# Two selects over every other column in place of a select in runs of two, with a new order of the steps

## The chip, the cores and the metric

One core of one Trainium2 chip runs the whole program. The metric is the device time in microseconds. The engines named below are PE (TensorE), DVE (VectorE), ACT (ScalarE), POOL (GpSimd) and SP (the queue that issues the DMAs).

## The reference

A gated delta-rule attention layer, then a mixture-of-experts layer, each followed by a residual and a layer norm. The input is 4 sequences of 512 tokens with 256 features. There are 16 key heads and 32 value heads of width 128.

```python
mixed = silu(causal_conv(hidden @ w_qkv, conv_w))        # 4 taps
q, k, v = split(mixed);  q, k repeated for 2 value heads each
g = -exp(A_log) * softplus(a + dt_bias);  beta = sigmoid(b)
q, k = l2norm(q) * DK ** -0.5, l2norm(k)
for t in range(S):                                       # per value head
    state = state * exp(g[t])
    delta = (v[t] - k[t] @ state) * beta[t]
    state = state + outer(k[t], delta)
    o[t] = q[t] @ state
o = rmsnorm(o * silu(hidden @ w_z)) * norm_gamma
x = layernorm(x + o @ w_out)
x = layernorm(x + moe(rmsnorm(x)))                       # 8 experts, top 2, and a shared one
```

## The kernel before

The recurrence over time is done in chunks of 128 tokens. Within a chunk it becomes the inverse of a 128 x 128 triangular matrix, and between chunks a 128 x 128 state is carried. A *body* is one key head of one sequence: 4 chunks times 2 value heads, which are 8 *cells*. There are 16 x 4 = 64 bodies (`BODIES`). The mixture of experts comes after them.

A body goes through these steps. `proj` multiplies the input with the weights of q, k and v; `tap` (ACT) and `conv` (DVE, twelve per body) are the four taps of the convolution, `silu` its activation. `ktp` and `vtp` are transposes on PE, `squares` and `kn` give the norms, `gate` and `zs` the output gate. `products` forms k k^T and q k^T. `diag` (POOL) and `scan` (DVE) make the decay matrix, and `m` and `p` (DVE) multiply the products with it.

The matrix m32T is then inverted for all 8 cells together. `mhi` (POOL, two halves) writes its fp16 copy mhiT with ones on the diagonal. `pairs` (POOL) writes the inverse of the 2 x 2 blocks on the diagonal to XT, and `x0` (DVE) transposes XT to X. Six levels follow (block sizes 2 to 64, i = 0 to 5): `join i` on PE and on DVE gives N, `growx i` on PE and ACT gives the new X, and XT is made anew by a DVE transpose (`turned`, levels 0 and 1) or by `growt` on PE and ACT (levels 2 to 5). `newton`, `res`, `finish` and `tt` correct the result once and give TT; `mlo` (POOL) is the low half of the matrix for that.

With TT the four chunks are gone through in order: `read`, `rhs`, `solve`, `u`, `write`, `s`, and `out` for the output. Then `og`, `power`, `pow`, `ogs`, `turn`, `project` and `acc` gate, normalise and project the output and add it up.

Work of three bodies is interleaved. The order is written out by hand in `ORDER`, one list per engine; an entry is (step, i, ahead). `rounds` goes through a list once for every k, and the entry works on body k + ahead. Each engine executes its list strictly in order, and semaphores hold the engines together. So a step that waits holds up everything behind it in its engine's list. One pass of a list is called a round here.

The names and lines that matter below: `conv` L1125, `proj` L870, `gate` L894, `products` L904, `join` L914 on PE and L1161 on DVE, `growx` L924 and L1075, `growt` L930 and L1078, `m` L1137, `mhi` L796, `pairs` L810 and L815, `x0` L1152, `turned` L1155, `mlo` L802 and L804, `squares` L1052, `solve` L965, `write` L975, `rhs` L1179.

Of the kernel before, what the change touches and what calls it, by code (L numbers as in the profile page):

```python
# [17 lines left out]
CELLS = CH * VH  # L18
# [10 lines left out]

ORDER = {  # L30
    "tensor": [
        ("read", 2, 0), ("growx", 0, 1), ("gate", 1, 1), ("gate", 2, 1), ("join", 1, 1), ("gate", 3, 1),
        ("growx", 1, 1), ("proj", 0, 2), ("proj", 1, 2), ("join", 2, 1), ("solve", 2, 0), ("proj", 2, 2),
        ("growx", 2, 1), ("growt", 2, 1), ("proj", 3, 2), ("join", 3, 1), ("write", 2, 0), ("out", 0, 0),
        ("growx", 3, 1), ("ktp", 0, 2), ("read", 3, 0), ("growt", 3, 1), ("join", 4, 1), ("out", 1, 0),
        ("growx", 4, 1), ("solve", 3, 0), ("growt", 4, 1), ("out", 2, 0), ("join", 5, 1), ("out", 3, 0),
        ("growx", 5, 1), ("growt", 5, 1), ("proj", 4, 2), ("newton", 0, 1), ("ktp", 1, 2), ("proj", 5, 2),
        ("newton", 1, 1), ("finish", 0, 1), ("proj", 6, 2), ("finish", 1, 1), ("proj", 7, 2), ("solve", 0, 1),
        ("products", 0, 2), ("write", 0, 1), ("products", 1, 2), ("turn", 0, 0), ("read", 1, 1), ("turn", 1, 0),
        ("project", 0, 0), ("project", 1, 0), ("solve", 1, 1), ("project", 2, 0), ("project", 3, 0), ("vtp", 0, 2),  # L40
        ("write", 1, 1), ("vtp", 1, 2), ("join", 0, 2), ("gate", 0, 2),
    ],
    "scalar": [
        ("u", 1, 0), ("silu", 2, 1), ("silu", 3, 1), ("vals", 0, 1), ("vals", 1, 1), ("growx", 0, 1), ("zs", 0, 1),
        ("growx", 1, 1), ("zs", 1, 1), ("tap", 0, 2), ("u", 2, 0), ("growx", 2, 1), ("growt", 2, 1), ("silu", 0, 2),
        ("tap", 1, 2), ("growx", 3, 1), ("squares", 0, 2), ("growt", 3, 1), ("kraw", 0, 2), ("u", 3, 0),
        ("growx", 4, 1), ("growt", 4, 1), ("power", 0, 0), ("growx", 5, 1), ("silu", 1, 2), ("growt", 5, 1),
        ("squares", 1, 2), ("tap", 2, 2), ("power", 1, 0), ("u", 0, 1), ("tap", 3, 2), ("turn", 0, 0), ("turn", 1, 0),
    ],
    "vector": [  # L50
        ("join", 2, 1), ("conv", 0, 2), ("conv", 1, 2), ("conv", 2, 2), ("join", 3, 1), ("s", 2, 0), ("conv", 3, 2),
        ("join", 4, 1), ("rhs", 3, 0), ("og", 0, 0), ("conv", 4, 2), ("conv", 5, 2), ("join", 5, 1), ("scan", 0, 2),
        ("scan", 1, 2), ("res", 0, 1), ("og", 1, 0), ("res", 1, 1), ("tt", 0, 1), ("tt", 1, 1), ("conv", 6, 2),
        ("conv", 7, 2), ("conv", 8, 2), ("s", 0, 1), ("conv", 9, 2), ("m", 0, 2), ("m", 1, 2), ("rhs", 1, 1),
        ("conv", 10, 2), ("conv", 11, 2), ("p", 0, 2), ("p", 1, 2), ("x0", 0, 2), ("acc", 0, 0), ("s", 1, 1),
        ("join", 0, 2), ("rhs", 2, 1), ("turned", 0, 2), ("join", 1, 2), ("acc", 1, 0), ("turned", 1, 2),
    ],
    "pool": [
        ("eq", 0, 1), ("mlo", 0, 1), ("qe", 0, 1), ("keys", 0, 1), ("kn", 0, 2), ("diag", 0, 2), ("pow", 0, 0),
        ("ogs", 0, 0), ("ogs", 1, 0), ("mhi", 0, 2), ("mhi", 1, 2), ("pairs", 0, 2),  # L60
    ],
}

# [10 lines left out]
def build_kernel(nc, x_rows, x_cols, w_heads, w_ab, conv_w, dt_bias, a_log, gamma, w_out,  # L74
                 rms_w, router_w, gate_up, down, tri, levels16, neg_mask, ident16, iota8, exponents, out):
    ctx = ExitStack()
    with ctx:
# [3 lines left out]
        def sem(name):  # L81
            return ctx.enter_context(nc.semaphore(name))
# [18 lines left out]
        acc = sb("acc", [P, TILES, D])  # L101
# [7 lines left out]
        conv = sb("conv", [P, GROUPS, SEQ])  # L109
# [20 lines left out]
        mhiT = sb("mhiT", [P, CELLS, P], F16)  # L130
# [591 lines left out]
        def _(pool):  # L722
# [18 lines left out]
            def run(name, i, n):  # L741
# [42 lines left out]
                elif name == "qe":  # L784
                    pool.wait_ge(s_silu, 4 * n + 2)
                    pool.wait_ge(s_ec[p], 16 * (n // 2 + 1))
                    if n > 1:
                        pool.wait_ge(s_pup, 2 * (n - 1))
                    pool.tensor_tensor(qE[:, p, VH:].rearrange("p (c v) n -> p c v n", v=VH),
                                       qT[:, p, P:].rearrange("p (c n) -> p c n", n=P).unsqueeze(2).broadcast_to([P, CH - 1, VH, P]),  # L790
                                       ecb[:, p, VH * P:].rearrange("p (c v n) -> p c v n", v=VH, n=P), ALU.mult).then_inc(s_qe, 1)
                elif name == "mhi":
                    pool.wait_ge(s_m, 2 * n + i + 1)
                    if n > 0:
                        pool.wait_ge(s_resp, 2 * n)
                    pool.affine_select(out=half(mhiT, i), in_=half(m32T, i), compare_op=ALU.not_equal, fill=1.0,  # L796
                                       base=0, pattern=[[0, 4], [-1, P]], channel_multiplier=1).then_inc(s_mhi, 1)
                elif name == "mlo":
                    pool.wait_ge(s_mhi, 2 * n + 2)
                    if n > 0:  # L800
                        pool.wait_ge(s_newp, 2 * n)
                    pool.tensor_tensor(mloT[:, :, :], m32T[:, :, :], mhiT[:, :, :], ALU.subtract).then_inc(s_mdif, 1)  # L802
                    pool.wait_ge(s_mdif, n + 1)
                    pool.affine_select(out=mloT[:, :, :], in_=mloT[:, :, :], compare_op=ALU.not_equal, fill=-2.0,  # L804
                                       base=0, pattern=[[0, CELLS], [-1, P]], channel_multiplier=1).then_inc(s_mlo, 1)
                elif name == "pairs":
                    pool.wait_ge(s_mhi, 2 * n + 2)
                    if n > 0:
                        pool.wait_ge(s_new, 2 * n)
                    pool.affine_select(out=XT[:, :, :].rearrange("p x (b j) -> p x b j", j=2),  # L810
                                       in_=mhiT[:, :, :].rearrange("p x (b j) -> p x b j", j=2), compare_op=ALU.is_equal, fill=0.0,
                                       base=0, pattern=[[0, CELLS], [-2, P // 2], [0, 2]], channel_multiplier=1).then_inc(s_near, 1)
                    odd = XT[:, :, :].rearrange("p x (b j) -> p x b j", j=2)[:, :, :, 1]
                    pool.wait_ge(s_near, n + 1)
                    pool.affine_select(out=odd, in_=odd, compare_op=ALU.not_equal, fill=1.0,  # L815
                                       base=-1, pattern=[[0, CELLS], [-2, P // 2]], channel_multiplier=1).then_inc(s_pair, 1)
                elif name == "pow":
                    if n == BODIES - 1:
                        for k in (1, 5):
                            prepare_pool(pool, k, 0)  # L820
                    pool.wait_ge(s_ms, 8 * n + 8)
                    pool.wait_ge(s_epsq, n + 1)
                    if n > 0:
                        pool.wait_ge(s_msl, n)
                    pool.tensor_tensor(by_chunk(ms[:, 1, :]), by_chunk(ms[:, 0, :]),  # L825
                                       epsq[:, n % 4].unsqueeze(2).broadcast_to([P, CH, VH]), ALU.add).then_inc(s_mse, 1)
                    pool.wait_ge(s_mse, n + 1)
                    if n > 0:
                        pool.wait_ge(s_on, 2 * n)
                    pool.tensor_tensor(ms[:, 2, :], ms[:, 1, :], expo[:, 0:1].broadcast_to([P, CELLS]),  # L830
                                       ALU.pow).then_inc(s_msl, 1)
# [275 lines left out]
        def _(dve):  # L1107
# [7 lines left out]
            def run(name, i, n):  # L1115
# [30 lines left out]
                                      bank4(I1)[:, 2 * i:2 * i + 2].unsqueeze(2).broadcast_to([P, 2, VH, P]),  # L1146
                                      half(decb, i).rearrange("p (c v) t -> p c v t", v=VH), ALU.mult).then_inc(s_p, 1)
                elif name == "x0":
                    dve.wait_ge(s_pair, n + 1)
                    if n > 0:  # L1150
                        dve.wait_ge(s_resp, 2 * n)
                    dve.transpose(flat(X), flat(XT)).then_inc(s_x0, 1)  # L1152
# [121 lines left out]
```

## Time and profile before

| | us |
|---|---|
| median of 3 runs (2604.12 to 2604.3) | 2604.27 |
| profiled execution, time | 2603.33 |
| profiled execution, span | 2601.6 |
| PE busy | 2379.1 (91%) |
| DVE busy | 1987.8 (76%) |
| POOL busy | 1417.4 (54%) |
| ACT busy | 1359.8 (52%) |
| mean granted PE clock | 0.967 |

The span goes from the first to the last instruction of the profiled execution; its time has something more around it. Busy times are shares of the span. The granted clock is the clock that PE was given, as a part of its full speed. Matrix multiplies are pipelined on PE: the start of the next one tells more of their cost than their own duration.

### The profile page before, as it was taken

The numbers are of one execution on the slowest core, as the hardware profiler recorded it, in microseconds if no ns is written. First come the engines' busy times: TensorE is split into PE (matmuls) and PEld (weight loads), VectorE is DVE, ScalarE is ACT, GpSimd is POOL, SyncE is SP. The second block draws the span as 40 slices with busy tenths as digits, with TensorE's granted clock in tenths as the row PEclk, the third lists the DMA queues.
The fourth block names the chain that finished last, engine by engine and source line by source line (L and its number), as shares of the span: only waits on it lengthen the run. The fifth ranks groups of instructions, "written<-read, shape, count | busy, mean of one in ns | idle before, by whom it ended". The sixth has DMA issues, their size and how long they took to land.

```text
span 2601.6 us, 54037 instructions
## 1 busy us (share of the span) xinstructions
PE 2379.1 (91%) x20078; PEld 1827.1 (70%) x20078; DVE 1987.8 (76%) x3452; ACT 1359.8 (52%) x4123; POOL 1417.4 (54%) x1198
## 2 busy tenths in 40 slices
PE   5899999999999999999999999999999999997998
PEld 3677777777777777777777777777777777775665
DVE  4778778777887777877778777887778877784665
ACT  3555565555555555555555555555555555553110
POOL 3465655656555665556655566555666556662000
PEclk9899999999999999999999999999999999998999
DMA  3011010101010100101010101101010110001000
GB/s 125 34 42 34 33 42 34 42 34 47 28 50 25 50 34 26 50 29 46 34 42 34 46 29 35 41 34 50 26 50 26 50 34 26 34 2 71 25 9 17
DMA packets 32100, 98.47 MB, mean 38 GB/s; under 512 B 4320, under 2 KB 9824, under 8 KB 31584
## 3 DMA queue, kind: packets, MB, share of 16 engines
q1 hardware_dynamic: 31840, 95.02, 10.6%
q8 instruction: 161, 2.64, 0.4%
q14 instruction: 99, 0.81, 0.1%
HBM read 92.39 MB, written 2.62 MB: 37 GB/s over the span
## 4 chain that ended last, share of the span: by engine, by line
PE 70%; POOL 16%; DVE 8%; issue 4%; ACT 0%; POOLq 0%; DMA 0%; DVEq 0%; SPq 0%; ACTq 0%
PE bank L870 18%; POOL XT L810 11%; PE bank L894 11%; PE bank L992 4%; PE bank L924 4%; PE bank L965 4%; PE bank L914 4%; PE bank L991 4%; PE bank L482 4%; DVE X L1152 3%; PE bank L953 3%; POOL mhiT L796 3%; PE bank L975 2%; PE bank L930 2%; PE bank L878 2%
## 5 line engine op out<-in xcount | busy, mean ns | idle before, releaser
L1125 DVE SCALAR_TENSOR_TENSOR conv<-bank,cw_all,conv 128x511 f32<-128x511 f32 (+2 forms) x768 | 571.4, 744 | 19.6 <-ACT conv L1030 6.0
L870 PE MATMUL bank<-xT,w_kh 128*128 128x512 f32 x1024 | 537.7, 618 | 2.7 <-ACT kraw L1058 1.8
L1075 ACT ACTIVATE X<-bank 128x512 f16<-128x512 f32 x384 | 228.9, 596 | 449.2 <-PE bank L924 435.8
L1161 DVE TENSOR_TENSOR N<-bank,lev 128x512 f16<-128x512 f32 x384 | 264.8, 690 | 107.3 <-PE bank L914 97.6
L914 PEld LDWEIGHTS bank<-X,mhiT 128*128 128x128 f16 x3072 | 132.3, 98 | 262.8 <-DVE X L1152 179.6
L750 POOL TENSOR_SCALAR ss<-ssum 128x4 f32<-128x4 f32 x64 | 14.6, 228 | 544.2 <-ACT sqj L1052 544.2
L894 PE MATMUL bank<-w_kh,xT 128*128 128x256 f32 x1024 | 310.0, 442 | 0.0
L914 PE MATMUL bank<-X,mhiT 128*128 128x64 f16 x3072 | 154.3, 194 | 165.6 <-DVE X L1152 164.2
L810 POOL TENSOR_SCALAR_AFFINE_SELECT XT<-mhiT 128x1024 f16<-128x1024 f16 x64 | 287.2, 4487 | 4.4
L1007 PE MATMUL bank<-wo,ogT 128*128 128x256 f32 x1024 | 246.8, 384 | 0.0
L1152 DVE STREAM_TRANSPOSE X<-XT 128x1024 f16<-128x1024 f16 x64 | 79.7, 1245 | 208.4 <-POOL XT L815 208.4
L1083 ACT ACTIVATE U<-bank 128x256 f32<-128x256 f32 x256 | 98.1, 383 | 243.7 <-PE bank L965 239.3
L894 PEld LDWEIGHTS bank<-w_kh,xT 128*128 128x128 f32 x1024 | 206.6, 218 | 24.8
L1155 DVE STREAM_TRANSPOSE XT<-X 128x1024 f16<-128x1024 f16 x128 | 159.4, 1245 | 62.6 <-ACT X L1075 62.6
L1007 PEld LDWEIGHTS bank<-wo,ogT 128*128 128x128 f32 x1024 | 185.7, 191 | 22.7
L1030 ACT ACTIVATE conv<-bank,cw_all 128x512 f32<-128x512 f32 x256 | 175.5, 686 | 48.5 <-PE bank L870 48.3
L924 PEld LDWEIGHTS bank<-N,XT 128*128 128x128 f16 x3072 | 130.8, 101 | 84.4 <-DVE N L1161 45.5
L825 POOL TENSOR_TENSOR ms<-ms,epsq 128x8 f32<-128x8 f32 x64 | 12.7, 198 | 322.3 <-ACT og L1090 322.3
L992 PE MATMUL bank<-U,pT 128*128 128x128 f32 x1024 | 187.7, 275 | 0.0
L870 PEld LDWEIGHTS bank<-xT,w_kh 128*128 128x128 f32 x1024 | 160.8, 192 | 36.2 <-issue 33.1
L1131 DVE TENSOR_TENSOR_SCAN decb<-egb,decb 128x512 f32<-128x512 f32 x128 | 149.7, 1211 | 46.7 <-POOL decb L774 46.7
L924 PE MATMUL bank<-N,XT 128*128 128x64 f16 x3072 | 162.6, 198 | 3.9 <-DVE N L1161 2.7
(160 smaller groups left out, 5859.7 us busy)
## 6 DMA issues: line engine op xcount, KB each, us to landing
egb<-rows SPq DMA_DIRECT2D x64, 512.0 KB, 3.6
ecb<-rows SPq DMA_DIRECT2D x64, 512.0 KB, 3.7
w_kh<-w_heads SPq DMA_DIRECT2D x16, 768.0 KB, 4.8
wo_raw<-w_out SPq DMA_DIRECT2D x16, 256.0 KB, 5.1
xT<-x_cols SPq DMA_DIRECT2D x4, 512.0 KB, 5.9
qT<-x_rows SPq DMA_DIRECT2D x4, 512.0 KB, 3.6
xT<-gate_up SPq DMA_DIRECT2D x1, 2048.0 KB, 7.5
out<-og SPq DMA_DIRECT2D x4, 512.0 KB, 3.0
```

Source lines behind the costliest of these rows:

```text
L810: pool.affine_select(out=XT[:, :, :].rearrange("p x (b j) -> p x b j", j=2), in_=mhiT[:, :, :].rearrange("p x (b j) -> p x b j", j=2), com ...
L870: mm = pe.matmul(PB[j % 2][:, :], w[:, k, g * P:(g + 1) * P], xT[:, k, b * SEQ:(b + 1) * SEQ], start=(k == 0), stop=(k == KT - 1))
L894: mm = pe.matmul(PB[h][:, 256 * c:256 * c + 256], xT[:, k, t * P:(t + 1) * P], w[:, k, 512:768], start=(k == 0), stop=(k == KT - 1))
L914: mm = pe.matmul(IB[1 - i % 2][:, x * 64:(x + 1) * 64], mhiT[:, x, :], blocks(X[:, x:x + 1, :], i, 0), start=True, stop=True)
L924: mm = pe.matmul(IB[i % 2][:, x * 64:(x + 1) * 64], XT[:, x, :], blocks(N[:, i, x:x + 1, :], i, 0), start=True, stop=True)
L992: mm = pe.matmul(dst, pT[:, p, x, :], U[:, x, :], start=(c == 0), stop=True)
L1007: mm = pe.matmul(OB[h][:, 256 * c:256 * c + 256], ogT[:, 2 * i + v, :], wo[:, head % 2, v, :], start=(v == 0), stop=(v == VH - 1))
L1030: act.activation(conv[:, g, :], PB[i % 2][:, :], ACT.Copy, scale=cw_all[:, head, g * TAPS + 3:g * TAPS + 4]).then_inc(s_tap, 1)
L1075: act.activation(blocks(X[:, :, :], i, 0), packed(IB[i % 2], i), ACT.Copy).then_inc(s_x, 1)
L1125: dve.scalar_tensor_tensor(conv[:, g, m:], PB[j % 2][:, 0:SEQ - m], cw_all[:, head, g * TAPS + 3 - m:g * TAPS + 4 - m], conv[:, g, m:], op ...
L1155: dve.transpose(flat(XT), flat(X)).then_inc(s_xv, 1)
L1161: dve.tensor_tensor(blocks(N[:, i], i, 0), packed(IB[1 - i % 2], i), blocks(lev[:, 1 + i:2 + i, :], i, 0).broadcast_to(shape), ALU.mult).t ...
```

## The change

Two things are changed.

First, `pairs`. Before, one select kept both columns 2b and 2b+1 of mhiT in row 2b and filled all else with 0; its access pattern ends in an inner run of two. A second select over the odd columns of the result then wrote 1 at (2b+1, 2b+1), after a wait for the first. Now two selects, one for the even and one for the odd columns, keep mhiT in the rows from 2b on and fill the rows above with 0. The matrix is zero below its diagonal and has ones on it, so the same values come out. Each reads and writes every other column, 512 elements a partition, and they don't wait for each other. The semaphore `s_near` goes, and `x0` waits for a count of `s_pair` that is twice as high.

Second, the four lists of `ORDER` are new. The set of steps is the same, and every engine executes each step once per body as before; their places and bodies ahead differ.

```diff
 ORDER = {
     "tensor": [
-        ("read", 2, 0), ("growx", 0, 1), ("gate", 1, 1), ("gate", 2, 1), ("join", 1, 1), ("gate", 3, 1),
-        ("growx", 1, 1), ("proj", 0, 2), ("proj", 1, 2), ("join", 2, 1), ("solve", 2, 0), ("proj", 2, 2),
-        ("growx", 2, 1), ("growt", 2, 1), ("proj", 3, 2), ("join", 3, 1), ("write", 2, 0), ("out", 0, 0),
-        ("growx", 3, 1), ("ktp", 0, 2), ("read", 3, 0), ("growt", 3, 1), ("join", 4, 1), ("out", 1, 0),
-        ("growx", 4, 1), ("solve", 3, 0), ("growt", 4, 1), ("out", 2, 0), ("join", 5, 1), ("out", 3, 0),
-        ("growx", 5, 1), ("growt", 5, 1), ("proj", 4, 2), ("newton", 0, 1), ("ktp", 1, 2), ("proj", 5, 2),
-        ("newton", 1, 1), ("finish", 0, 1), ("proj", 6, 2), ("finish", 1, 1), ("proj", 7, 2), ("solve", 0, 1),
-        ("products", 0, 2), ("write", 0, 1), ("products", 1, 2), ("turn", 0, 0), ("read", 1, 1), ("turn", 1, 0),
-        ("project", 0, 0), ("project", 1, 0), ("solve", 1, 1), ("project", 2, 0), ("project", 3, 0), ("vtp", 0, 2),
-        ("write", 1, 1), ("vtp", 1, 2), ("join", 0, 2), ("gate", 0, 2),
+        ("newton", 1, 0), ("vtp", 1, 1), ("finish", 0, 0), ("gate", 0, 1), ("finish", 1, 0), ("gate", 1, 1),
+        ("products", 0, 1), ("solve", 0, 0), ("products", 1, 1), ("write", 0, 0), ("proj", 0, 2), ("read", 1, 0),
+        ("out", 0, 0), ("proj", 1, 2), ("solve", 1, 0), ("gate", 2, 1), ("write", 1, 0), ("gate", 3, 1),
+        ("join", 0, 1), ("read", 2, 0), ("out", 1, 0), ("growx", 0, 1), ("solve", 2, 0), ("proj", 2, 2),
+        ("write", 2, 0), ("join", 1, 1), ("proj", 3, 2), ("read", 3, 0), ("ktp", 0, 2), ("growx", 1, 1),
+        ("solve", 3, 0), ("out", 2, 0), ("out", 3, 0), ("join", 2, 1), ("proj", 4, 2), ("ktp", 1, 2), ("proj", 5, 2),
+        ("growx", 2, 1), ("growt", 2, 1), ("proj", 6, 2), ("join", 3, 1), ("proj", 7, 2), ("growx", 3, 1),
+        ("turn", 0, 0), ("growt", 3, 1), ("join", 4, 1), ("turn", 1, 0), ("project", 0, 0), ("growx", 4, 1),
+        ("growt", 4, 1), ("project", 1, 0), ("join", 5, 1), ("project", 2, 0), ("growx", 5, 1), ("growt", 5, 1),
+        ("project", 3, 0), ("vtp", 0, 2), ("newton", 0, 1),
     ],
     "scalar": [
...
+        ("silu", 2, 1), ("growt", 4, 0), ("silu", 3, 1), ("growx", 5, 0), ("growt", 5, 0), ("vals", 0, 1),
+        ("zs", 0, 1), ("u", 0, 0), ("vals", 1, 1), ("tap", 0, 2), ("u", 1, 0), ("zs", 1, 1), ("growx", 0, 1),
+        ("u", 2, 0), ("silu", 0, 2), ("power", 0, 0), ("tap", 1, 2), ("kraw", 0, 2), ("u", 3, 0), ("growx", 1, 1),
+        ("squares", 0, 2), ("silu", 1, 2), ("power", 1, 0), ("squares", 1, 2), ("growx", 2, 1), ("tap", 2, 2),
+        ("growt", 2, 1), ("growx", 3, 1), ("turn", 0, 0), ("tap", 3, 2), ("growt", 3, 1), ("turn", 1, 0),
+        ("growx", 4, 1),
     ],
     "vector": [
...
+        ("p", 1, 1), ("rhs", 1, 0), ("x0", 0, 1), ("conv", 0, 2), ("s", 1, 0), ("conv", 1, 2), ("join", 0, 1),
+        ("rhs", 2, 0), ("conv", 2, 2), ("og", 0, 0), ("turned", 0, 1), ("s", 2, 0), ("join", 1, 1), ("rhs", 3, 0),
+        ("conv", 3, 2), ("conv", 4, 2), ("conv", 5, 2), ("og", 1, 0), ("turned", 1, 1), ("join", 2, 1),
+        ("join", 3, 1), ("conv", 6, 2), ("conv", 7, 2), ("join", 4, 1), ("conv", 8, 2), ("conv", 9, 2),
+        ("conv", 10, 2), ("join", 5, 1), ("conv", 11, 2), ("scan", 0, 2), ("acc", 0, 0), ("res", 0, 1), ("res", 1, 1),
+        ("tt", 0, 1), ("tt", 1, 1), ("scan", 1, 2), ("m", 0, 2), ("m", 1, 2), ("acc", 1, 0), ("s", 0, 1), ("p", 0, 2),
     ],
     "pool": [
-        ("eq", 0, 1), ("mlo", 0, 1), ("qe", 0, 1), ("keys", 0, 1), ("kn", 0, 2), ("diag", 0, 2), ("pow", 0, 0),
-        ("ogs", 0, 0), ("ogs", 1, 0), ("mhi", 0, 2), ("mhi", 1, 2), ("pairs", 0, 2),
+        ("kn", 0, 1), ("diag", 0, 1), ("mhi", 0, 1), ("mhi", 1, 1), ("pairs", 0, 1), ("mlo", 0, 1), ("eq", 0, 1),
+        ("keys", 0, 1), ("qe", 0, 1), ("pow", 0, 0), ("ogs", 0, 0), ("ogs", 1, 0),
     ],
 }
...
-                    pool.affine_select(out=XT[:, :, :].rearrange("p x (b j) -> p x b j", j=2),
-                                       in_=mhiT[:, :, :].rearrange("p x (b j) -> p x b j", j=2), compare_op=ALU.is_equal, fill=0.0,
-                                       base=0, pattern=[[0, CELLS], [-2, P // 2], [0, 2]], channel_multiplier=1).then_inc(s_near, 1)
-                    odd = XT[:, :, :].rearrange("p x (b j) -> p x b j", j=2)[:, :, :, 1]
-                    pool.wait_ge(s_near, n + 1)
-                    pool.affine_select(out=odd, in_=odd, compare_op=ALU.not_equal, fill=1.0,
-                                       base=-1, pattern=[[0, CELLS], [-2, P // 2]], channel_multiplier=1).then_inc(s_pair, 1)
+                    for j in range(2):
+                        pool.affine_select(out=XT[:, :, :].rearrange("p x (b j) -> p x b j", j=2)[:, :, :, j],
+                                           in_=mhiT[:, :, :].rearrange("p x (b j) -> p x b j", j=2)[:, :, :, j],
+                                           compare_op=ALU.is_ge, fill=0.0, base=0, pattern=[[0, CELLS], [-2, P // 2]],
+                                           channel_multiplier=1).then_inc(s_pair, 1)
...
-                    dve.wait_ge(s_pair, n + 1)
+                    dve.wait_ge(s_pair, 2 * n + 2)
```

## Rows read from the trace of the kernel before

**Rows 1.** The page: busy time of the engines, and the chain's shares by engine.

```profile
PE 2379.1 (91%) x20078; PEld 1827.1 (70%) x20078; DVE 1987.8 (76%) x3452; ACT 1359.8 (52%) x4123; POOL 1417.4 (54%) x1198
...
PE 70%; POOL 16%; DVE 8%; issue 4%; ACT 0%; POOLq 0%; DMA 0%; DVEq 0%; SPq 0%; ACTq 0%
```

**Rows 2.** Waits by total: who waited for whom, us in total, times, longest.

```profile
DVE X L1152 <- POOL XT L815: 208.4, 64, 3.7
...
PE bank L914 <- DVE X L1152: 164.2, 64, 3.5
```

**Rows 3.** The chain that ended last: start us, us, what.

```profile
1068.36 0.64 POOL mhiT L796
...
1069.05 4.50 POOL XT L810
...
1074.47 1.25 DVE X L1152
```

**Rows 4.** Stretches: length, busy us (instructions) of each engine, PEclk, DMA share, GB/s.

```profile
1003.57:1040.74 37.17, 34.18 (x302) 26.75 (x303) 28.81 (x48) 20.54 (x63) 22.46 (x20) 0.95 0.08 30
1040.74:1075.77 35.03, 32.58 (x302) 25.53 (x303) 28.81 (x48) 20.54 (x63) 21.50 (x19) 1.00 0.20 61
1075.77:1079.00 3.23, 3.23 (x23) 2.56 (x24) 2.07 (x6) 0.02 (x1) 3.08 (x3) 0.60 0.02 5
```

**Rows 5.** Line 1152: duration ns min/median/max, first and last start; and one start.

```profile
L1152 DVE STREAM_TRANSPOSE X<-XT x64: 1244/1245/1247, 62.1 to 2336.9; 128x1024 f16<-128x1024 f16 x64
...
100.87 1.24 DVE L1152 STREAM_TRANSPOSE X<-XT 128x1024 f16<-128x1024 f16 x1 [3.12 <-POOL XT L815]
```

**Rows 6.** Groups on POOL: busy us, mean ns, idle before.

```profile
L810 POOL TENSOR_SCALAR_AFFINE_SELECT XT<-mhiT 128x1024 f16<-128x1024 f16 x64 | 287.2, 4487 | 4.4
...
L804 POOL TENSOR_SCALAR_AFFINE_SELECT mloT<-mloT 128x1024 f16<-128x1024 f16 x64 | 69.9, 1091 | 9.8 <-POOL mloT L802 0.4
L815 POOL TENSOR_SCALAR_AFFINE_SELECT XT<-XT 128x512 f16<-128x512 f16 x64 | 48.3, 755 | 9.2
```

**Rows 7.** Timeline of PE: start us, us, what, count.

```profile
1044.72 1.10 PE L894 MATMUL bank<-w_kh,xT 128*128 128x256 f32 x4
1045.67 0.41 PE L924 MATMUL bank<-N,XT 128*128 128x64 f16 x8
1045.91 1.96 PE L870 MATMUL bank<-xT,w_kh 128*128 128x512 f32 x4
1047.71 0.40 PE L914 MATMUL bank<-X,mhiT 128*128 128x64 f16 x8
...
1064.32 1.06 PE L904 MATMUL bank<-kT 128*128 128x128 f32 x8
1065.21 0.61 PE L975 MATMUL bank<-U,keys 128*128 128x128 f32 x4
1065.65 1.06 PE L904 MATMUL bank<-qT,kT 128*128 128x128 f32 x8
```

**Rows 8.** Timeline of DVE, same columns.

```profile
1043.50 1.25 DVE L1155 STREAM_TRANSPOSE XT<-X 128x1024 f16<-128x1024 f16 x1 [0.32 <-ACT X L1075]
...
1063.63 2.31 DVE L1125 SCALAR_TENSOR_TENSOR conv<-bank,cw_all,conv 128x511 f32<-128x511 f32 x3
1065.86 0.49 DVE L1189 COPY S<-bank 128x128 f32<-128x128 f32 x2
...
1066.92 1.28 DVE L1137 TENSOR_TENSOR m32T<-bank,decb 128x512 f32<-128x512 f32 x2
1068.11 0.60 DVE L1179 SCALAR_TENSOR_TENSOR rhs<-bank,sc_all,vals 128x128 f32<-128x128 f32 x2
```

**Rows 9.** Timeline of ACT, same columns.

```profile
1042.87 0.60 ACT L1075 ACTIVATE X<-bank 128x512 f16<-128x512 f32 x1 [4.24 <-PE bank L924]
...
1052.87 0.27 ACT L1052 ACTIVATE sqj<-bank 128x128 f16<-128x128 f32 x1
...
1053.78 0.23 ACT L1052 ACTIVATION_READ_ACCUMULATOR sqj<-bank 128x1 f32 x1
```

More of the change, by code:

```diff
@@ L42 @@
+        ("growx", 2, 1), ("growt", 2, 1), ("proj", 6, 2), ("join", 3, 1), ("proj", 7, 2), ("growx", 3, 1),
+        ("turn", 0, 0), ("growt", 3, 1), ("join", 4, 1), ("turn", 1, 0), ("project", 0, 0), ("growx", 4, 1),
+        ("growt", 4, 1), ("project", 1, 0), ("join", 5, 1), ("project", 2, 0), ("growx", 5, 1), ("growt", 5, 1),
+        ("project", 3, 0), ("vtp", 0, 2), ("newton", 0, 1),
     ],
     "scalar": [
-        ("u", 1, 0), ("silu", 2, 1), ("silu", 3, 1), ("vals", 0, 1), ("vals", 1, 1), ("growx", 0, 1), ("zs", 0, 1),
@@ L45 @@
[L45 to L48, printed above, removed]
+        ("silu", 2, 1), ("growt", 4, 0), ("silu", 3, 1), ("growx", 5, 0), ("growt", 5, 0), ("vals", 0, 1),
@@ L49 @@
+        ("zs", 0, 1), ("u", 0, 0), ("vals", 1, 1), ("tap", 0, 2), ("u", 1, 0), ("zs", 1, 1), ("growx", 0, 1),
[3 more added lines that the diff above has]
+        ("growx", 4, 1),
     ],
     "vector": [
-        ("join", 2, 1), ("conv", 0, 2), ("conv", 1, 2), ("conv", 2, 2), ("join", 3, 1), ("s", 2, 0), ("conv", 3, 2),
@@ L52 @@
[L52 to L56, printed above, removed]
+        ("p", 1, 1), ("rhs", 1, 0), ("x0", 0, 1), ("conv", 0, 2), ("s", 1, 0), ("conv", 1, 2), ("join", 0, 1),
@@ L192, in build_kernel @@
         s_mlo = sem("s_mlo")
-        s_near = sem("s_near")
         s_pair = sem("s_pair")
```

## The prediction

> **What bounds the kernel now.** I read the page first: PE is busy for 91% of the span, and the chain that ended last lies on PE for 70% and on POOL for 16% [rows 1]. So two things want explaining: what PE does, and why POOL is on the path. The waits say it: DVE stood 208.4 us, 64 times, in front of the transpose `x0` until the second select of `pairs` was done, and PE stood 164.2 us, 64 times, for that transpose, which is 2.57 us a body [rows 2]. The chain in order of time shows the stretch: the last `mhi` 0.64, the first select of `pairs` 4.50, the second, then the transpose 1.25, at whose end `join 0` starts on PE [rows 3]. Apart from this one gap PE is packed: in the round from 1040.74 to 1075.77 it is busy for 32.58 of 35.03 us at a granted clock of 1.00, while DVE has 28.81, ACT 20.54 and POOL 21.50 us of work [rows 4]. The gap has a second price. Other rounds take 37.17 us at 0.95 with the same instructions, and right behind one gap the clock is 0.60 over 3.23 us, which is mostly the lower level (1.2 GHz of 2.4) [rows 4]. From the first transpose at 62.1 to the last at 2336.9 there are 63 rounds, so a mean one takes 2274.8/63 = 36.11 us [rows 5]; of its distance to 32.58, some 2.45 us are the gap and 1.08 us the lower clock after it.
>
> **The two selects.** The old pair costs 4.487 us for 1024 elements, in runs of two, and 0.755 us for 512 elements at every other column; with the start and the wait between them 5.40 us pass from 1069.05 to the transpose at 1074.47 [rows 3, 6]. The new pair is twice 512 elements at every other column of fp16, a form that differs from the 0.755 us one only in its comparison, its base and its separate input. I take 2 x 0.755 = 1.51 us. Neither waits for the other. Bounds: at the rate of the `mlo` select (1.091 us for 1024 contiguous elements, so 0.55 us for half) the pair would be 1.1 us; if the comparison or the second tile made each as dear as the old 1024-element one, it would be 2 x 4.487 = 8.97 us. I stay with the row that shares the access pattern. POOL's load falls by 3.7 us a round, which matters nowhere else.
>
> The GPSIMD Engine Reference of the Trainium skill (3.1, Elementwise) gives about 1.8 cycles per element, 768 ns for 512 elements; the 0.755 us row agrees, the 4.487 us row doesn't. By that rule alone the old pair would be three halves of the new one, and the change would take only some 0.8 us out of the chain instead of 3.9. The same page (section 7) warns of many small reads and advises to batch them into one access of more dimensions, which speaks against splitting; here the batched form is the dear one, so the rows decide.
>
> **What the new order makes of it.** The gap goes only if `join 0` finds its transpose ready, so I lay out the chain from `products 0` on. Slots, start to start: a `gate` 0.95, `join`/`growx`/`growt` 0.24, a `proj` 1.80/2 = 0.90, `products` 0.89, `write` 0.44 [rows 7]; `read`, `solve`, `out 0` about the same as `write`, taken as 0.48. In the old order PE starts `products 0` at 1064.32 and `join 0` 11.45 us later, at 1075.77 [rows 4, 7]. In the new order PE has between those two: `products` twice (1.78), `proj` twice (1.80), `gate` twice (1.90), and six small steps (`solve` 0 and 1, `write` 0 and 1, `read` 1, `out` 0: 2.9). So `join 0` is due 8.4 us after `products 0` starts.
> DVE, POOL and DVE against that: the product is out at 0.89 + about 0.2 = 1.1. Both `m` follow at once (in the old order a block of three `conv` and more stood in front of them, start 1066.92 for a product started at 1064.32): 1.28 us, out at 2.4 [rows 8]. `mhi 1` starts about 0.15 later and takes 0.64: 3.2. The new pair of selects: 4.75. On DVE there now stand between `m` and `x0`: `acc 1`, `s 0`, `p` twice, `rhs 1`. `m` holds DVE to 2.3, the others 0.6 + 0.4 + 1.2 + 0.5 us, and `rhs 1` must wait for `read 1`, so DVE is free at 5.1; that, not POOL, now starts the transpose. It is out at 6.4, and `join 0` due at 8.4 has about 1.9 us to spare. The pair of selects might even take 3.76 us before PE noticed. So the 2.45 us gap and the lower clock behind it go; with the old selects (5.24 and 0.1 between them) the new order would still wait 5.35 - 3.76 = 1.6 us there.
>
> **What is late next.** The floor of a round is PE's 32.58 us. Every engine takes its list in order, so I followed the new lists from hand to hand; a result takes about 0.04 us to the next engine (DVE leaves its turn at 1043.50, 0.03 us behind ACT's end at 1042.87 + 0.60) [rows 8, 9]. PE's steps before `join 2` sum to 20.1 us from `newton 1`. These come out late:
> `growx 2`, due at 22.6: its `join 2` on DVE stands behind `og 1`, which waits for `out 3` until 20.4, and a transpose of 1.25: done at 22.85, 0.2 late.
> `proj 6`, due at 23.3: it needs the bank that `squares 1` reads, and on ACT that stands behind `power 1`, which waits for the same `og 1`; with 1.1 us for four squares [rows 9] it ends at 23.45, 0.15 late.
> `join 4`: after `growx 3` PE has only a turn and a `growt`, 0.92 us in all, while the result comes back after 0.41 + 0.60 + handoffs = 1.1 us: 0.2 late.
> `growx 4`, `growx 5`, `newton 0` and `newton 1`: each some 0.08 late, the last two since `silu 3` stands before `growx 5` on ACT: 0.3.
> Together 0.85 us. About 0.3 us of such small waits are already in the 32.58, since a packed sum of all slots gives 32.3. I take 32.58 + 0.57 = 33.15 us a round. DVE then has 28.81 of 33.15 us, so it can take these turns but little more. Gaps of 0.2 us are a tenth of the one that brought the clock down, and I expect it at 1.00.
> PE's list issues the same instructions as before, and so do ACT's and DVE's; SP's loads wait for the same counts of the same semaphores as before, and of the PE, DVE or POOL waits above none was put down to a DMA, so I keep them hidden.
>
> **Ends.** In the first round the pair saves 3.9 us, but `products 0` of body 0 now stands behind `vtp 1` and two `gate` steps, about 4 us and more of PE and ACT at low load; the following round, 38.8 us long in the old order [rows 5], holds less work instead. I count a gain of 3.4 us over both, and 62 rounds from then on. Each of these took (2336.95 - 100.87)/62 = 36.07 us. The tail behind the last transpose (264.6 us, mostly the experts) stays.
>
> **Sum.** 62 x (36.07 - 33.15) = 181 us, and 3.4: 184 us. The profiled execution has a span of 2601.6 and a time of 2603.33, so 1.7 us lie around the span; it becomes 2419. The median of the runs is 0.9 us above the profiled one: 2420 us.
>
> **Rivals.**
> A. Better packed: the small waits don't appear, 32.5 us a round: 2420 - 62 x 0.65 = 2380. For it: PE's own sequence has the work; against it: the in-order queues above.
> B. The new order has a further turn that I took for hidden, 34.3 us a round: DVE at 28.8 us of work is the candidate, with `join 2` and `join 3` next to each other and every `conv` behind them. 2420 + 62 x 1.15 = 2491. Or the new select keeps the per-element price of the run of two, 4.487/2 = 2.24 us: the pair is 4.5 us, 0.7 beyond the slack, 2465.
> C. The change doesn't do what it says: the price lay in something that both forms share (the writing of XT from another tile), and the pair stays at 5.35 us. Then the gap shrinks to 1.6 us by the order alone, and the lower clock may stay: 33.15 + 1.6 + 1.08 = 35.8 us a round, 2584. Against it: the 0.755 us row writes XT as well.
> D. Slower than before: each strided select costs as much as the old one, 8.97 us for the pair, behind the same `mhi`. `join 0` is then 8.97 - 3.76 = 5.2 us late, a round is 33.15 + 5.2 + 1.08 = 39.4, and the time 2420 + 62 x 6.3 = 2810. It would be slower than before from a pair of about 5.6 us on (with the low clock; 6.7 without). For it: 4.487 us shows that one select can be that dear. Against it: its time went with the inner run of two, which is gone.
>
> **Numbers.** Forecast 0.66; A 0.12; B 0.15; C 0.02; D 0.05. That gives 0.94 faster, 0.01 within 0.2% (about what a measurement of this kernel can tell from no change) and 0.05 slower. The likeliest time is 2420. For 8 in 10 the range takes in A and B's second form (2465), and goes most of the way to its first: 2380 to 2480.
>
> **What would show it.** In the changed kernel's profile: two selects of about 0.75 us on the line of `pairs`, and none above 2; DVE's transpose `x0` released no more by POOL, or after a wait of little length; no wait of `join 0` for it on PE; a round of 33.1 us by the first and last start of the transpose; a granted clock of 1.00 in the rounds; small waits of PE for `join`'s N and for `growx`'s X, some 0.1 to 0.2 us each. I am wrong if the selects' mean isn't near 0.755, if one PE wait exceeds 0.5 us in each round, or if the clock still falls in the rounds.

## The result, and the profile after

The changed kernel takes 2392.14 us (median of 4 runs, 2391.15 to 2392.77), the kernel before 2604.19 us in the same comparison: a ratio of 0.9186, 95% interval 0.917 to 0.9201. That is 212 us less, where 184 were forecast (2420, range 2380 to 2480).

The page of the changed kernel, with the busy times, and below them the chain's shares by engine, which answer to [rows 1]:

```profile
PE 2329.1 (97%) x20078; PEld 1788.0 (75%) x20078; DVE 1969.7 (82%) x3452; ACT 1325.5 (55%) x4123; POOL 1175.9 (49%) x1198
...
PE 76%; POOL 11%; issue 8%; DVE 3%; ACT 1%; POOLq 0%; DMA 0%; SPq 0%; DVEq 0%; ACTq 0%
```

PE is busy for 97% of the span instead of 91%, and for 50 us less in all with the same count of instructions. That is the second price of the gap coming back. In the kernel before, 35 of the 62 rounds from body 1 on ran at a clock of 0.95 and 27 at 1.00, with PE busy for 34.18 us in the one kind and 32.58 in the other [rows 4]; in the changed kernel all 62 run at 1.00. POOL keeps 11% of the chain although hardly anything waits for it, so here the waits tell more than the chain.

The groups that write XT on POOL, the answer to [rows 6]: one line now, with the 128 selects of the new pair.

```profile
L811 POOL TENSOR_SCALAR_AFFINE_SELECT XT<-mhiT 128x512 f16<-128x512 f16 x128 | 92.6, 764 | 4.4
```

And the transpose `x0` (line 1150 now), with its waits: the answer to [rows 2] and [rows 5].

```profile
L1150 DVE STREAM_TRANSPOSE X<-XT x64: 1229/1231/1245, 65.5 to 2124.6; 128x1024 f16<-128x1024 f16 x64
...
  POOL XT L811: 1.1, 1
...
  PE bank L912: 0.6, 1
```

Of the 64 waits of DVE for POOL one is left, of 1.1 us, in the first round; 208.4 us of them had been there. PE's 164.2 us are 0.6. A stretch from one transpose to the next, for [rows 4]:

```profile
1013.45:1046.09 32.64, 32.64 (x304) 25.59 (x303) 28.52 (x48) 20.08 (x63) 17.72 (x19) 1.00 0.09 33
```

PE is busy in all of the 32.64 us, at the full clock. From 65.5 to 2124.6 there are 63 rounds, 32.68 us each instead of 36.11.

How the chain from `products 0` to `join 0` came out, on PE, DVE and POOL (timelines: start, us, engine, what). PE:

```profile
1008.34 1.16 PE L902 MATMUL bank<-kT 128*128 128x128 f32 x8
...
1016.35 0.40 PE L912 MATMUL bank<-X,mhiT 128*128 128x64 f16 x8
1016.59 0.68 PE L951 MATMUL bank<-S,kT 128*128 128x256 f32 x2
```

DVE:

```profile
1009.53 1.29 DVE L1135 TENSOR_TENSOR m32T<-bank,decb 128x512 f32<-128x512 f32 x2
...
1013.45 1.23 DVE L1150 STREAM_TRANSPOSE X<-XT 128x1024 f16<-128x1024 f16 x1
1014.64 0.75 DVE L1123 SCALAR_TENSOR_TENSOR conv<-bank,cw_all,conv 128x511 f32<-128x511 f32 x1
1015.68 0.61 DVE L1189 SCALAR_TENSOR_TENSOR S<-S,sc_all,bank 128x128 f32<-128x128 f32 x2 [0.29 <-PE bank L973]
```

POOL:

```profile
1010.38 1.23 POOL L796 TENSOR_SCALAR_AFFINE_SELECT mhiT<-m32T 128x512 f16<-128x512 f32 x2 [7.68 <-DVE m32T L1135]
1011.67 1.45 POOL L811 TENSOR_SCALAR_AFFINE_SELECT XT<-mhiT 128x512 f16<-128x512 f16 x2
```

`products 0` starts at 1008.34. The prediction had `m` at +1.1, the pair ready at +4.75, DVE free at +5.1, the transpose out at +6.4 and `join 0` at +8.4. They came at +1.2, +4.8 (1011.67 + 1.45), +5.1, +6.3 and +8.0. Nothing waits for POOL any more; DVE's own list starts the transpose.

The ledger, from the starts of the transpose (body 0, body 1, body 63) in both traces:

| stretch | before | after | difference | forecast |
|---|---|---|---|---|
| up to `x0` of body 1 | 100.87 | 98.31 | -2.6 | -3.4 |
| 62 rounds | 62 x 36.07 | 62 x 32.68 | -209.8 | -181 |
| behind the last `x0` | 264.6 | 266.4 | +1.8 | 0 |

### The profile page after: what moved, and what is told of

Same layout as the page of the kernel before. It is cut to its first block, busy times and chain, and to the rows that moved or that the text cites. A ratio compares the mean times of both kernels' runs of the same rounds, so it can differ in the third digit from the quotient of the medians.

```text
span 2391.0 us, 53973 instructions
## 1 busy us (share of the span) xinstructions
PE 2329.1 (97%) x20078; PEld 1788.0 (75%) x20078; DVE 1969.7 (82%) x3452; ACT 1325.5 (55%) x4123; POOL 1175.9 (49%) x1198
## 4 chain that ended last, share of the span: by engine, by line
PE 76%; POOL 11%; issue 8%; DVE 3%; ACT 1%; POOLq 0%; DMA 0%; SPq 0%; DVEq 0%; ACTq 0%
PE bank L868 15%; PE bank L892 8%; PE bank L1005 8%; PE bank L902 4%; PE bank L482 4%; PE bank L963 4%; PE bank L990 4%; PE bank L922 3%; PE bank L912 3%; PE bank L951 3%; PE bank L973 3%; PE bank L989 3%; PE bank L996 2%; PE bank L520 2%; PE bank L928 2%
## 5 line engine op out<-in xcount | busy, mean ns | idle before, releaser
L868 PE MATMUL bank<-xT,w_kh 128*128 128x512 f32 x1024 | 550.2, 620 | 3.2 <-ACT sqj L1050 2.3
L796 POOL TENSOR_SCALAR_AFFINE_SELECT mhiT<-m32T 128x512 f16<-128x512 f32 x128 | 78.8, 637 | 494.2 <-DVE m32T L1135 494.2
L1005 PE MATMUL bank<-wo,ogT 128*128 128x256 f32 x1024 | 280.2, 397 | 0.0
L892 PE MATMUL bank<-w_kh,xT 128*128 128x256 f32 x1024 | 271.8, 389 | 0.1
L1069 ACT ACTIVATE zs<-bank 128x512 f32<-128x512 f32 x128 | 76.4, 597 | 289.8 <-PE bank L892 289.8
L922 PEld LDWEIGHTS bank<-N,XT 128*128 128x128 f16 x3072 | 123.2, 98 | 128.6 <-DVE N L1159 109.2
L892 PEld LDWEIGHTS bank<-w_kh,xT 128*128 128x128 f32 x1024 | 176.4, 192 | 14.6 <-issue 0.5
L1005 PEld LDWEIGHTS bank<-wo,ogT 128*128 128x128 f32 x1024 | 176.5, 192 | 13.7
L868 PEld LDWEIGHTS bank<-xT,w_kh 128*128 128x128 f32 x1024 | 155.9, 192 | 18.5 <-issue 4.0
L990 PEld LDWEIGHTS bank<-U,pT 128*128 128x128 f32 x1024 | 156.2, 193 | 3.3
L1088 ACT ACTIVATE og<-og 128x128 f32<-128x128 f32 x512 | 151.0, 297 | 11.1 <-DVE og L1196 5.4
```

What stands on the lines that cost most here:

```text
L868: mm = pe.matmul(PB[j % 2][:, :], w[:, k, g * P:(g + 1) * P], xT[:, k, b * SEQ:(b + 1) * SEQ], start=(k == 0), stop=(k == KT - 1))
L892: mm = pe.matmul(PB[h][:, 256 * c:256 * c + 256], xT[:, k, t * P:(t + 1) * P], w[:, k, 512:768], start=(k == 0), stop=(k == KT - 1))
L922: mm = pe.matmul(IB[i % 2][:, x * 64:(x + 1) * 64], XT[:, x, :], blocks(N[:, i, x:x + 1, :], i, 0), start=True, stop=True)
L990: mm = pe.matmul(dst, pT[:, p, x, :], U[:, x, :], start=(c == 0), stop=True)
L1005: mm = pe.matmul(OB[h][:, 256 * c:256 * c + 256], ogT[:, 2 * i + v, :], wo[:, head % 2, v, :], start=(v == 0), stop=(v == VH - 1))
```

## The experiments

Two questions stood open. Which of the two edits brought the gain? And what of the chain's reckoning holds: the price of a select, the time to spare at `join 0`, and the small waits that were to make a round 33.15 us? Times are medians; each ratio is to the kernel before, run on the same chip.

### Each half alone

The new pair with the old lists:

```diff
 ORDER = {
-    (the four lists of the changed kernel)
+    (the four lists of the kernel before)
 }
```

> Old order of all four lists, new pair of selects alone. Theory (the order is not needed for the gain, the select's price is the whole of it): in the old order m comes out at 1068.20, the second mhi at 69.0, the new pair at 70.5, but DVE is held by p until 71.3, so the transpose is out at 72.5, and join 0, due at 73.16, never waits. A round takes 32.4 to 32.6 us, the time is 2604.2 - 63 x (36.11 - 32.5) = 2377, between 2370 and 2395. Rival (the order carries a part): once the gap of 2.5 us is gone, waits come out that it covered, above all the second gate behind vals on ACT, which in the old trace ends at 74.2, and acc; each up to 1 us: a round of 33.5, 2440.

Measured: 2366.49 us, ratio 0.9086 (0.9071 to 0.9101). So this kernel is faster than the changed one by 26 us, and just under the range of its own theory. A second measurement of it:

> Old order with the new pair of selects once more, beside the kernel with one select. 2366 again, a ratio to before of 0.908 to 0.910; if it comes out at 2390, the 26 us by which the old order was ahead were not its own.

Measured: 2366.51 us, ratio 0.9086 (0.9073 to 0.9098), against 0.9186 for the changed kernel: the intervals lie apart. A round of the old order with the new pair:

```profile
1063.15:1095.51 32.36, 32.36 (x304) 25.74 (x303) 28.82 (x48) 20.54 (x64) 18.20 (x20) 1.00 0.20 66
```

The mean round, over the 62 behind the transpose of body 1 (91.22 to 2098.98), takes 32.38 us, 0.3 less than in the new order. The rival's waits behind the gap did not come out. At the start of the round before it, the transpose on DVE:

```profile
1030.74 1.23 DVE L1149 STREAM_TRANSPOSE X<-XT 128x1024 f16<-128x1024 f16 x1
```

and the last `vtp` and `join 0` on PE:

```profile
1032.26 0.60 PE L883 MATMUL bank<-tri_sb,vT 128*128 128x128 f32 x4
1032.69 0.40 PE L911 MATMUL bank<-X,mhiT 128*128 128x64 f16 x8
```

The transpose ends at 1031.97 and `join 0` starts at 1032.69, 0.43 us behind the `vtp` before it. That is the slot of a `vtp`, so nothing stood between them.

The other half: the old pair with the new lists.

```diff
-                    for j in range(2):
-                        pool.affine_select(... is_ge, every other column ...)
+                    (the two selects of the kernel before, with s_near between them)
...
-                    dve.wait_ge(s_pair, 2 * n + 2)
+                    dve.wait_ge(s_pair, n + 1)
```

> New order, old pair of selects. Theory: the transpose starts 8.7 us after products 0 instead of 5.1, is out at 10.0, and join 0 was due at 8.0: 2.0 us late. A round is 34.65 us with the clock at 1.00 and up to 1.1 more where the clock falls after the gap: 2515 to 2585, a granted clock in the rounds of 0.95 to 1.00. Rival (the order by itself brings a large part, the selects little): below 2450.

Measured: 2676.83 us, ratio 1.027 (1.0253 to 1.0287). Neither theory had this: the new order alone makes the kernel slower. Its waits in total (who waited for whom, us, times, longest), DVE for POOL:

```profile
DVE X L1153 <- POOL XT L816: 229.8, 64, 5.1
```

and PE for DVE:

```profile
PE bank L915 <- DVE X L1153: 123.7, 64, 4.6
PE bank L954 <- DVE S L1192: 49.1, 65, 2.7
```

`join 0` waits 123.7/64 = 1.9 us a round, as worked out. But a second wait stands behind it: `read 2` waits for `s 1`. In the new DVE list `s 1` stands behind the transpose and a `conv`, so a late transpose makes `s 1` late as well. And the clock:

```profile
884.49:921.91 37.42, 34.75 (x302) 26.99 (x302) 28.70 (x47) 20.07 (x64) 22.48 (x20) 0.95 0.09 29
...
996.44:1032.17 35.73, 33.11 (x302) 25.49 (x302) 28.46 (x48) 20.01 (x64) 21.49 (x19) 1.00 0.09 31
```

The rounds at a clock of 1.00 take 35.73 us, the others some 1.5 more, and only 9 of the 63 are short ones.

### What the two halves give together

| | old pair | new pair |
|---|---|---|
| old order | 2604.2 | 2366.5 |
| new order | 2676.8 | 2392.1 |

The pair is worth 238 us in the old order and 285 in the new one. The order costs 73 us with the old pair and 26 with the new one. The whole gain of the change is the pair's; the order takes some of it back.

### What makes a select dear

One select instead of two in the new order, with the new comparison and the old pattern:

```diff
-                    for j in range(2):
-                        ... [:, :, :, j] ..., pattern=[[0, CELLS], [-2, P // 2]]
+                    pool.affine_select(out=XT ... "p x (b j) -> p x b j", in_=mhiT ... "p x (b j) -> p x b j",
+                                       compare_op=ALU.is_ge, ..., pattern=[[0, CELLS], [-2, P // 2], [0, 2]])
```

> New order, but one select (the new comparison, keep in rows from 2b on) over all 1024 elements in the old access pattern with the inner run of two; the same values. Theory (the inner run makes the price): 4.49 us for the select, the transpose 3.0 us later than with the new pair, of which 2.0 are to spare, join 0 1.0 us late: a round of 33.7, with some lower clock up to 34.7: 2455 to 2520. Rival (the comparison is_equal, or the fill of most elements, made it dear): 1.5 us or less, 2392.

And one select in which the two columns are the outermost dimension:

```diff
+                    pool.affine_select(out=XT ... "p x (b j) -> p j x b", in_=mhiT ... "p x (b j) -> p j x b",
+                                       compare_op=ALU.is_ge, ..., pattern=[[0, 2], [0, CELLS], [-2, P // 2]])
```

> New order, one select over the same 1024 elements with the two columns of a pair as the outermost dimension and 64 blocks as the innermost (every other element); the same values. Theory (only the inner run of two is dear): 1.4 to 1.5 us in one instruction, time 2392 as with two. Rival (a third dimension of the pattern or 1024 elements from one tile to another is dear): near 4.5 us, 2455 to 2520.

Measured: 2569.99 us (0.9863, 0.9847 to 0.988) and 2392.26 us (0.9181, 0.9166 to 0.9197). The select in the first:

```profile
L810 POOL TENSOR_SCALAR_AFFINE_SELECT XT<-mhiT 128x1024 f16<-128x1024 f16 x64 | 286.9, 4483 | 4.4
```

and in the second, busy us and mean ns behind the bar:

```profile
L810 POOL TENSOR_SCALAR_AFFINE_SELECT XT<-mhiT 128x1024 f16<-128x1024 f16 x64 | 85.7, 1340 | 4.4
```

The same comparison, tiles, elements and number of dimensions cost 4.483 us with the run of two inside and 1.340 us with it outside. So the inner run makes the price, and neither the comparison nor the count of dimensions. Whether it is the run's length of two or its pattern step of 0 that costs was not separated. The time of the first was forecast too low by 50 us and more; its PE waits show why:

```profile
PE bank L911 <- DVE X L1149: 65.9, 64, 3.7
PE bank L950 <- DVE S L1188: 49.2, 65, 2.7
```

`join 0` is 1.0 us late (65.9/64), as expected, and `read 2` another 0.76 us (49.2/65), which was left out. The clock fell to 0.95 in 24 of the 62 rounds from body 1 on.

### How much time the transpose really has

Each select issued twice, in the new order:

```diff
-                    for j in range(2):
+                    for j in (0, 1, 2, 3):
+                        if j == 2:
+                            pool.wait_ge(s_pair, 4 * n + 2)
                         ... [:, :, :, j % 2] ...
...
-                    dve.wait_ge(s_pair, 2 * n + 2)
+                    dve.wait_ge(s_pair, 4 * n + 4)
```

> New order, each of the two new selects issued twice with a wait between the pairs; the same values. The pair takes 3.0 us instead of 1.45, the transpose starts 1.2 us later. Theory of the prediction (join 0 alone counts, which has 2.0 us to spare from POOL): no change, 2392. Theory after the runs with the old select (s 1 stands behind the transpose and a conv on DVE, and read 2 on PE waits for it, with only 0.5 us to spare): read 2 comes 0.65 us late in every round, and PE's drain of 0.16 is bare too: 2392 + 63 x 0.65 to 0.8 = 2433 to 2443.

Measured: 2435.45 us, ratio 0.9355 (0.9338 to 0.9372). The theory of the prediction falls, the second one's number comes. One wait of PE in each round:

```profile
1001.80 0.40 PE L914 MATMUL bank<-X,mhiT 128*128 128x64 f16 x8
1002.57 0.70 PE L953 MATMUL bank<-S,kT 128*128 128x256 f32 x2 [0.37 <-DVE S L1191]
```

`join 0` doesn't wait, `read 2` does: it starts 0.77 us after `join 0`, against 0.24 in the changed kernel (1016.35 to 1016.59). That is 0.5 of the 0.67 us by which a mean round is longer (33.35 instead of 32.68); the rest was not followed. So `join 0` had the time that I gave it, but another step had less. A wait of 0.37 us alone does not bring the clock down: over 150 to 2050 us it is 1.00.

```profile
150.00:2050.00 1900.00, 1876.87 (x17201) 1457.38 (x17198) 1620.55 (x2678) 1139.05 (x3591) 1105.84 (x1155) 1.00 0.12 41
```

The same doubling in the old order:

> Old order, each of the two new selects issued twice with a wait between the pairs. POOL is 0.7 us ahead of DVE in the old order with the new pair, so the transpose comes 0.8 us later and join 0, which follows it by 0.05 us less than nothing to spare on PE, 0.15 to 0.9 us late. Theory (the old order has about 0.7 us to spare on join 0, none of it more): 0.1 to 0.3 us a round, 2370 to 2385. Rival (join 0 stands just at its transpose, no slack left): 0.8 us a round, 2417.

Measured: 2391.74 us, ratio 0.9186 (0.9169 to 0.9203), 25 us above the old order with the pair issued once, between the two theories. In its trace three rounds in four take 32.63 us and the fourth 33.18, where there were 32.35 and 32.42. Every fourth round POOL also scales the weights of the next head (`ogs 1`, 1.04 us) ahead of `mhi`. So the old order stands nearly at its edge too: with the new pair POOL is 0.7 us ahead of DVE there, and DVE's transpose 0.7 us ahead of `join 0`; the doubling takes 1.5. By this sum `join 0` is only 0.1 us late, while the round is 0.28 us longer; the rest was not followed.

To see that `s 1` behind the transpose is the cause, the old pair in the new order, with `s 1` before it:

```diff
-        ("rhs", 1, 0), ("x0", 0, 1), ("conv", 0, 2), ("s", 1, 0), ("conv", 1, 2), ...
+        ("rhs", 1, 0), ("s", 1, 0), ("x0", 0, 1), ("conv", 0, 2), ("conv", 1, 2), ...
```

> New order and old pair of selects with one exchange on DVE: s 1 before the transpose x0 and the conv instead of behind them. Theory (of the 4.6 us a round that the old pair costs in the new order, 0.73 are the wait of read 2 for s 1, and 0.16 PE's drain before it): the wait of read 2 goes, that of join 0 (1.9 us) stays: 0.9 us a round less, 2676.8 - 57 = 2620, less if the clock falls in fewer rounds. Rival (read 2's wait lies inside other waits, or a later one takes its place): 2665 or more.

Measured: 2598.61 us, ratio 0.9981 (0.9971 to 0.9991): 78 us less than with `s 1` behind. PE's waits, in total:

```profile
PE bank L915 <- DVE X L1153: 123.8, 64, 4.6
...
PE bank L954 <- DVE S L1192: 3.9, 3, 2.7
```

The wait of `read 2` is gone (3.9 of 49.1 us are left), and that of `join 0` is the same to 0.1 us. The time is 21 us below the theory's 2620. The mechanism is shown, but not the size: the rounds at full clock take 35.33 us instead of 35.73, so 0.4 less and not 0.9. A part came back as a wait of `growx 0` for the N of `join 0`, which `read 2` had covered:

```profile
935.26 0.39 PE L993 MATMUL bank<-U,pT 128*128 128x128 f32 x2
935.85 0.41 PE L925 MATMUL bank<-N,XT 128*128 128x64 f16 x8 [0.20 <-DVE N L1162]
```

The other 0.8 us a round are the clock's. Here 30 of the 62 rounds from body 1 on are slow ones and take 1.0 us more, where 53 of 62 had taken 1.5 more. In the slow rounds `growx 0` does not wait, which is a part of why they cost less here. The stretch of rounds with `s 1` in front (the clock is the third column from the end):

```profile
150.00:2250.00 2100.00, 1983.74 (x17727) 1534.09 (x17726) 1682.05 (x2751) 1178.98 (x3700) 1269.55 (x1068) 0.98 0.11 38
```

and with `s 1` behind the transpose:

```profile
150.00:2350.00 2200.00, 2044.59 (x17965) 1586.65 (x17963) 1703.78 (x2791) 1195.45 (x3765) 1289.78 (x1086) 0.96 0.11 36
```

### The small waits

> New order and new pair with one exchange on PE: turn 1 before join 4 instead of after it. Theory (the small waits are what makes the new order's round longer than the old one's; here join 4 waits 0.15 us for ACT's X of level 3): 63 x 0.15 = 9 us less, 2383. Rival (the wait only moves, since turn 1 then waits for POOL or growx 4 for join 4): 2390 to 2395.

```diff
-        ("turn", 0, 0), ("growt", 3, 1), ("join", 4, 1), ("turn", 1, 0), ("project", 0, 0), ...
+        ("turn", 0, 0), ("growt", 3, 1), ("turn", 1, 0), ("join", 4, 1), ("project", 0, 0), ...
```

Measured: 2391.18 us, ratio 0.9187 (0.9171 to 0.9204): no change. The wait can be read off PE's starts. In the changed kernel `growt 3` holds PE 0.38 us where `growt` 4 and 5 hold it 0.24:

```profile
1027.58 0.40 PE L928 MATMUL bank<-XT,N 128*128 128x64 f16 x8
1027.93 1.13 PE L868 MATMUL bank<-xT,w_kh 128*128 128x512 f32 x2
...
1030.79 0.40 PE L928 MATMUL bank<-XT,N 128*128 128x64 f16 x8
1031.17 0.41 PE L912 MATMUL bank<-X,mhiT 128*128 128x64 f16 x8
...
1031.89 1.03 PE L1005 MATMUL bank<-wo,ogT 128*128 128x256 f32 x4
1032.82 0.39 PE L922 MATMUL bank<-N,XT 128*128 128x64 f16 x8
```

With the exchange `turn 1` starts 0.24 us after `growt 3` does, but the `project` after `join 4` then takes 1.06 us to the next step instead of 0.93:

```profile
1028.91 0.40 PE L928 MATMUL bank<-XT,N 128*128 128x64 f16 x8
1029.15 0.66 PE L996 MATMUL bank<-tri_sb,og 128*128 128x128 f32 x4
...
1029.88 1.11 PE L1005 MATMUL bank<-wo,ogT 128*128 128x256 f32 x4
1030.94 0.39 PE L922 MATMUL bank<-N,XT 128*128 128x64 f16 x8
```

The wait moved on to `growx 4`. Taking away one such wait is worth nothing while the next step of the same chain of levels comes no sooner.

Last, the single select in the old order:

> Old order, and the pair made by one select with the two columns outermost (1.34 us instead of 1.45 for two). Theory (in the old order DVE, held by p, starts the transpose, 0.7 us after POOL is done, so 0.1 us on POOL is worth nothing): the same as the old order with two selects, 2366. Rival (a launch less on POOL shortens the round): 2360 or less.

Measured: 2367.72 us, ratio 0.9089 (0.9077 to 0.9102), the same as with two. The best version found is the old order with the new pair, in either form.

## Why the prediction was right

**The select's price.** Right: 1.45 us for the pair (1.51 forecast), and its reason, the inner run, is shown by the two single selects. The 5.40 us read off [rows 3] for the old pair are 5.42, which changes nothing. The Trainium skill's GPSIMD Engine Reference (3.1, Elementwise) has 1.8 cycles an element as its best case, from which 1.54 us for 1024 elements is an estimate. 1.34 and 1.45 us were measured, somewhat below that, and 4.48 for the same count with the run of two, of which that section says nothing. The advice of section 7 of that reference in the Trainium skill, to batch small reads into one access, is worth 0.1 us here, the distance between two selects and one with the columns outside. With the run of two inside, one select costs 3.0 us more than two.

**The gap and the clock.** Right: no wait of `join 0` but one of 0.6 us at the start, a clock of 1.00 in the rounds. Each point of the chain came within 0.4 us of its place, the transpose within 0.1.

**The round.** 32.68 us, forecast 33.15: the mis-sized terms of the sum. The floor of 32.58 was PE's busy time in a round that ended in a gap. It holds the drain of the last matmul, the end of its duration that the next one otherwise overlaps and that is bare only where a gap follows. The last step before the gap of [rows 4]'s round, in the timeline of the kernel before:

```profile
1072.28 0.61 PE L975 MATMUL bank<-U,keys 128*128 128x128 f32 x4
1072.72 0.60 PE L886 MATMUL bank<-tri_sb,vT 128*128 128x128 f32 x4
1075.77 0.41 PE L914 MATMUL bank<-X,mhiT 128*128 128x64 f16 x8 [2.45 <-DVE X L1152]
```

The `vtp` lasts 0.60 us and the step after such a group of four starts 0.44 behind its start, so 0.16 us of the 32.58 come from the gap itself. The ends of matmuls are modelled in the profile, but whole rounds agree. With the single select in runs of two, a round at full clock is 2.2 us longer than in the changed kernel, 34.86 against 32.68, and the two waits in it sum to 1.8, which leaves 0.2 for each gap. The old order without the gap runs at 32.38 us. And the new order stands 0.3 us above that, not 0.57. The wait for `squares 1` (0.12 us, the slot of 0.35 before 1027.93) and that of `join 4` (0.15) were there as forecast; that of `growx 2` for `join 2` shrank from 0.2 to 0.05. So of the error of 0.47 us a round, 0.2 is the floor and 0.15 the wait for `join 2`; the remaining 0.1 lies among the small waits of `growx` 4 and 5 and of `newton` and was not separated. 62 x 0.47 = 29 us covers the whole error of 28; the two ends, 0.8 and 1.8 us worse than forecast, and what lies outside the span account for the small remainder.

**What I had wrong and the time did not show.** The pair could not take 3.76 us unnoticed. I gave the time to spare at `join 0` as that of the transpose, but the transpose also holds up all that stands behind it on DVE. For `s 1` and `read 2` POOL had only about 0.9 us to spare: 0.3 in which the pair was ready before DVE, 0.29 in which `s 1` waited for `write 1` (the row at 1015.68), and 0.25 from the end of `s 1` at 1016.29 to `read 2` at 1016.59, handoff taken off. With the pair at 1.45 us the forecast did not depend on it. But the rivals did, and with them the upper part of the range. The second form of B, a pair of 4.5 us, was priced at 2465, and the kernel with a select of 4.48 us took 2570. Rival C, 2584 by that sum, is the new order with the old pair, which took 2677. And D put the point where the change makes the kernel slower at a pair of 5.6 us, while the old pair of 5.4 was already 73 us slower. All three left out `read 2`, and B's second form the clock as well.

**What I did not ask.** The prediction worked out the new order with both pairs, and never the old order with the new pair. The trace of the kernel before had all of it, though [rows 3, 7, 8] show only a part: `m` out at 1068.20, POOL's pair at 70.5, DVE free of `p` at 71.3, the transpose out at 72.5, `join 0` due at 73.16. The new order was not needed for the gain, and costs 26 us. Between the two profiled executions (2391.0 and 2364.1 us of span) it is 7.1 us up to the transpose of body 1, 62 x 0.30 = 18.5 after that, and 1.3 behind the last. At the start it puts two `gate` steps and `vtp` before the first product, which comes at 60.78 instead of 51.18, so that the first transpose starts at 65.49 instead of 57.14 in the old order. The gates and the first product on PE in the changed kernel:

```profile
57.29 3.65 PE L892 MATMUL bank<-w_kh,xT 128*128 128x256 f32 x8
60.78 1.05 PE L902 MATMUL bank<-kT 128*128 128x128 f32 x8
```

and in the old order with the new pair:

```profile
51.18 1.05 PE L901 MATMUL bank<-kT 128*128 128x128 f32 x8
```

What exactly makes the new order's round 0.3 us longer is shown only in part. Its list leaves PE short gaps of 0.1 to 0.15 us at three or four places of the levels, and moving one did nothing. The slots of PE's steps, start to start and summed over the 62 rounds of both traces, say where the time goes. A round of the new order spends 0.42 us more than the old one on the slots of `growt` and `join`, where those gaps are, 0.26 more on `project` (0.94 each instead of 0.88), and 0.1 more each on `products` and `vtp`. It spends 0.35 less on `out`, and 0.1 less each on `gate` and the first `solve`. So not all of it is waits: the same step is dearer or cheaper behind another neighbour, as a `proj` starting at 1018.75 behind a `solve` fills a slot of 0.86 us and one at 1020.30 behind a `join` 0.94. Whether a better list of this shape exists was not tried.

## What to carry to other kernels

Before an order is rewritten around a quicker step, run the step alone in the old order: here that was the better kernel. The time to spare in front of one waiter is not that of the instruction; go through everything queued behind it on its engine and take the least. And a busy time read from a round that ends in a gap holds the drain of a pipeline, so packed slots, start to start, are the floor.

## What the runs showed of the hardware

An affine select on POOL with an inner run of two elements took 4.48 us for 1024 fp16 elements a partition, 3.3 times the 1.34 us of the same work with the run outermost. One select of 1024 at every other element took 1.34 us, two of 512 took 1.45.

Behind the first rounds, the granted clock of PE fell only in kernels with longer waits of PE, and a round had a mean of either 1.00 or 0.95. Of the 62 rounds from body 1 on, none fell to 0.95 with one wait of 0.37 us in each (0.6 to 0.7 in four). With 0.98 and 0.73 us, their ends 1.1 us apart, 24 of 62 did; with 1.89 us alone or followed by 0.20, 30 did; with one of 2.1 to 3.0 us (the kernel before), 35; with 1.89 and 0.73, 53. A round in which the clock fell was 1.0 to 1.6 us longer. Two rounds of the kernel with one select and the run of two, the columns as in [rows 4]:

```profile
813.95:848.75 34.80, 33.09 (x304) 25.51 (x302) 28.45 (x47) 19.99 (x63) 20.77 (x18) 1.00 0.09 31
848.75:885.28 36.53, 34.76 (x304) 26.80 (x302) 28.66 (x47) 20.05 (x63) 21.76 (x19) 0.95 0.09 30
```
